# Extra matmuls into an unread PSUM bank while TensorE waits in two graph convolutions

## The chip, the cores and the metric

The kernel runs on one core of one Trainium2 chip. The metric is the device time of one execution, in microseconds (us), as the median of several runs.

## What is computed

Four graph layers stand one behind the other, on 6250 nodes with 128 features and 100000 edges that are sorted by their target. Each layer's result is added to its input and normalized over the features. The change lies in the fourth, two GCN convolutions with a relu between them:

```
def _gcn_layer(x, row, col, ew, W, b, n):
    deg = segment_sum(ew, col, num_segments=n)
    dis = where(deg > 0, rsqrt(maximum(deg, 1e-12)), 0.0)
    norm = dis[row] * ew * dis[col]
    h = x @ W
    msg = h[row] * norm[:, None]
    return segment_sum(msg, col, num_segments=n) + b

h = relu(_gcn_layer(x, row, col, ew, W1, b1, n))
out = _gcn_layer(h, row, col, ew, W2, b2, n)
x = layernorm(x + out)
```

The layers before it are an attention layer over the edges with a softmax (L0), one with four heads (L1), and an edge MLP (L2).

## The kernel before

The edges lie in 782 tiles of 128, the nodes in tiles of 128. Before each convolution a table `t3` or `t4` of all nodes' rows `dis * (x @ W)` is written to HBM. The convolution then does two things per edge: it fetches the row of the edge's source from the table, and it adds that row, times the edge weight, to the target's row.

The fetch is POOL's work. It issues one indirect DMA per tile of edges (line 2246, 128 rows of 128 floats), eight tiles to a group, 98 groups (`CTILE_GROUPS`), into a ring of 96 slots in SBUF (`conv_ring`, a part of `arena`). Before the gathers of group k, `landed` (line 1819) waits for group k - 2 and counts it in the semaphore `tiles_landed`; for the last groups `count_landed` (line 1812) does so.

The sum is PE's work. A step is one pair of a tile of edges and a tile of nodes that it touches; there are 832 such steps, in 104 groups of eight (`CSTEP_GROUPS`), which this document calls steps of PE where it speaks of one pass through `step`. PE multiplies a one-hot matrix of the targets (`hot8`, 128 x 128, with the edge weight as its one) with the fetched rows, and accumulates into one of three PSUM windows of 128 x 1024 floats (`pair[g % 3]`), at an offset that is read from a table. Each of the eight f32 matmuls shows as two records in the trace, 16 to a burst. Two small matmuls with zeros open the window (line 2290) and two close it (line 2299); the last one raises `summed`. PE waits for three things: that the window is cleared, that the one-hots are made, and that enough groups have landed, by a table `step_need` (lines 2289 to 2294).

DVE does four things per step: it builds the one-hots of the next step (TENSOR_SCALAR, line 2313, eight of them), adds the window to the accumulator of the nodes (TENSOR_TENSOR, line 2323), and clears the window (MEMSET, line 2326); the register of the first node is loaded ahead of them. ACT copies the next indices and weights (lines 2256 to 2261) once `summed` is raised, and raises `placed`. POOL's group k needs ACT's copies that were made at step k - 5 (`LAG`), so PE's and ACT's progress reaches POOL only at that distance.

Each engine's program is its own; semaphores alone tie them. `conv_rounds` (line 1798) writes the first twelve passes and the last eight out and makes a loop of twelve passes for those between. The bank `bank[7]`, the second half of `pair[3]`, is used by no engine in the two convolutions. The first one keeps a bias in the other half.

The constants are `ident_b`, the bf16 identity of 128 x 128, and `iota_b`, bf16 numbers 0 to 127 in each row.

Of the kernel before, what the change touches and what calls it, by code (L numbers as in the profile page):

```python
# [20 lines left out]
ALU = mybir.AluOpType  # L21
# [3 lines left out]
P = 128  # L25
# [19 lines left out]
CTILE_GROUPS = -(-ET // CG)  # L45
# [47 lines left out]
def build(nc, x, edge_i, edge_f, W_att_w, W_att_b, W1_w, W1_b, W2_w, W2_b, a_vec,  # L93
# [3 lines left out]
    with ctx:  # L97
        def sb(name, shape, dt=F32):
            return ctx.enter_context(nc.sbuf_tensor(name, shape, dt))
# [68 lines left out]
        iota_b = sb("iota_b", [P, P], BF16)  # L168
        ident = sb("ident", [P, P])
        ident_b = sb("ident_b", [P, P], BF16)  # L170
# [88 lines left out]
        bank = [pair[n // 2][:, (n % 2) * 512:(n % 2 + 1) * 512] for n in range(8)]  # L259
# [27 lines left out]
        v, s_, t_, q_ = nc.vector, nc.scalar, nc.tensor, nc.gpsimd  # L287
# [394 lines left out]
        def batch_rounds(eng, batch):  # L682

            batch(0, 0, 2)
            batch(1, 1, 2)
            with eng.Fori(2, NB - 2) as b:
                batch(b, 2, 2)
            batch(NB - 2, 2, 1)
            batch(NB - 1, 2, 0)  # L690

        NORM = BT + 1

# [50 lines left out]
        with nc.Block() as block:  # L744
# [301 lines left out]
            @block.tensor  # L1046
            def _(pe):
                turns = {at: (n, rows) for n, (at, rows, _) in enumerate(turned)}

                def turn(n, rows):  # L1050
# [51 lines left out]
        spare = wide[:, :, :, :].rearrange("p a b c -> p (a b c)")  # L1102
# [719 lines left out]

        def rows_of(eng, need, table, k):

            eng.reg_load([need], table[0:1, bass.ds(k, 1)])
            return eng.snap(need, min_val=0, max_val=CTILE_GROUPS - 1) + 1

        def at_least(eng, signal, k, more):

# [8 lines left out]
        with nc.Block() as block:  # L1838
# [134 lines left out]
            def _(dve):  # L1973
                first = [dve.alloc_register(f"l2_node{g}") for g in range(2)]
                slots = [dve.alloc_register(f"l2_slot{u}") for u in range(CG)]
                need = dve.alloc_register("l2_need")

                def hot_look(i, g, k):
                    dve.wait_ge(l2_rel_in[g % 4 // 2], 16 * (k // 4 + 1) if isinstance(k, int) else 4 * k - 4 * (g % 4) + 16)
# [253 lines left out]
        def convolution(name, table, table_out, also_act=None, also_dve=None):  # L2233
            placed, tiles_landed, hot_made, summed, added, cleared = (
                sem(f"{name}_{n}") for n in ("placed", "landed", "hot", "sum", "acc", "cleared"))
            with nc.Block() as block:
# [41 lines left out]
                @block.tensor  # L2278
                def _(pe):
                    slots = [pe.alloc_register(f"{name}_slot{u}") for u in range(CG)]  # L2280
                    offsets = [pe.alloc_register(f"{name}_offset{u}") for u in range(CG)]
                    need = pe.alloc_register(f"{name}_need")

                    def step(i, g, k):
                        window = pair[g % 3]
                        pe.reg_load(slots, step_slot[0:1, bass.ds(k * CG, CG)])
                        pe.reg_load(offsets, step_offset[0:1, bass.ds(k * CG, CG)])
                        pe.wait_ge(cleared, k + 1)
                        for h in range(2):
                            t_.matmul(window[:, h * 512:h * 512 + D], zeros[:, 0:P], zeros[:, 0:D], start=True, stop=False)  # L2290
                        pe.wait_ge(hot_made, k + 1)
                        pe.wait_ge(tiles_landed, rows_of(pe, need, step_need, k))
                        for u in range(CG):
                            slot = pe.snap(slots[u], min_val=0, max_val=CSLOTS - 1)
                            offset = pe.snap(offsets[u], min_val=0, max_val=CG - 1)
                            t_.matmul(window[:, bass.ds(offset * D, D)], hot8[:, g % 2, u, :], conv_ring[:, bass.ds(slot * D, D)],  # L2296
                                      start=False, stop=False)
                        for h in range(2):
                            last = t_.matmul(window[:, h * 512:h * 512 + 2], zeros[:, 0:P], zeros[:, 0:2], start=False, stop=True)  # L2299
                        last.then_inc(summed, 1)  # L2300

                    conv_rounds(pe, step, CSTEP_GROUPS)
# [210 lines left out]
```

## Time and profile before

| | |
|---|---|
| median of 3 runs | 6958.88 us |
| lowest, highest | 6939.15, 6967.73 us |
| profiled execution: span from its first to its last instruction | 5685.5 us |
| profiled execution: its own time | not recorded apart from its span |
| mean granted TensorE clock over the span | 0.647 |
| first convolution: first gather, last closing matmul | 3583.78, 4595.29 us |
| second convolution: last gather begins | 5631.8 us |

The median of the runs holds 1273 us that lie outside the span. Times in the trace count from the first instruction of the span. "PE" is a matmul on TensorE and "PEld" a weight load; "POOLq" is the instruction queue of GpSimd, in which its semaphore counts stand. PE, PEld, DVE, ACT and POOL overlap, and their shares are not to be added. The granted clock is given as a share of 2.4 GHz, so 0.50 is 1.2 GHz; a value between the two levels is a mean over a stretch in which it changed.

### The profile page before, as it was taken

What the parts mean: (1) busy time and instruction counts of PE and PEld (TensorE: products, weight loads), DVE (VectorE), ACT (ScalarE), POOL (GpSimd) and SP (SyncE); (2) the same over time, 40 slices, a digit from 0 to 9 for tenths busy, and PEclk for the clock granted to TensorE, in tenths of its full rate; (3) what the DMA queues carried; (4) which work ended last, traced back from release to release, by engine and by line L of the source; (5) the groups of instructions that cost most, each with busy time, mean ns of one, the idle gap of its engine ahead of it and who ended that gap; (6) DMA issues with size and microseconds to landing.
All of it is one profiled execution on the core that took longest, in us unless ns stands there. A gap on an engine that the chain in (4) does not pass through costs nothing. (4 is left out here: it accounts for less than half of the span.)

```text
span 5685.5 us, 82572 instructions
## 1 busy us (share of the span) xinstructions
PE 3113.8 (55%) x17051; PEld 2734.5 (48%) x17052; DVE 3263.6 (57%) x12090; ACT 1491.5 (26%) x5626; POOL 3958.0 (70%) x4054
## 2 busy tenths in 40 slices
PE   4444444356666666778898988433333443333333
PEld 3333333345555555657777776333333343333332
DVE  6888887676787787744444444433444443344445
ACT  2333333345555555532222223100000000000001
POOL 3777777736777777367777772677777757777774
PEclk7555555568888777865555556666666666666666
DMA  5111112214444444222121110111111121111112
GB/s 123 52 52 52 52 52 56 49 52 131 132 132 131 130 131 131 70 54 56 52 56 51 53 52 21 56 52 51 51 51 51 51 61 52 51 51 51 51 51 57
DMA packets 222234, 385.68 MB, mean 68 GB/s; under 512 B 85452, under 2 KB 121882, under 8 KB 221998
## 3 DMA queue, kind: packets, MB, share of 16 engines
q0 software_dynamic: 142944, 296.35, 19.0%
q1 hardware_dynamic: 79054, 86.72, 5.0%
q8 instruction: 83, 1.36, 0.1%
q14 instruction: 153, 1.25, 0.1%
HBM read 356.23 MB, written 26.56 MB: 67 GB/s over the span
## 5 line engine op out<-in xcount | busy, mean ns | idle before, releaser
L2246 POOL DMA_INDIRECT arena<-table_gcn,idx_now x1568 | 1532.2, 977 | 642.9 <-issue 422.1
L2296 PE MATMUL pair<-arena,hotf 128*128 x3328 | 726.6, 408 | 1224.7 <-POOLq L1819 1199.3
L2296 PEld LDWEIGHTS pair<-arena,hotf 128*128 128x128 f32 x3328 | 691.2, 317 | 1256.1 <-issue 1255.8
L664 POOL DMA_INDIRECT arena<-table_attention,idx_now x832 | 825.7, 992 | 272.7 <-issue 197.2
L664 POOL DMA_INDIRECT arena<-table_key_value,idx_now x832 | 789.2, 949 | 275.9 <-issue 221.1
L1852 POOL DMA_INDIRECT arena<-table_edge_mlp,idx_now x784 | 768.1, 980 | 261.2 <-issue 212.4
L2323 DVE TENSOR_TENSOR acc<-acc,pair 128x1024 f32 x208 | 253.9, 1221 | 1133.9 <-PE pair L2299 1133.9
L1069 PE MATMUL pair<-wide,hotf 128*128 128x130 f32 x1664 | 431.0, 439 | 653.3 <-ACT wide L1033 653.3
L1069 PEld LDWEIGHTS pair<-wide,hotf 128*128 128x128 f32 x1664 | 369.0, 326 | 718.5 <-ACT wide L1033 718.5
L2256 ACT COPY idx_now<-src_t 128x8 int32 (+1 forms) x204 | 39.3, 197 | 1815.2 <-PE pair L2299 1803.2
L1406 PE MATMUL pair<-wide,hotf 128*128 128x132 f32 x1664 | 314.1, 347 | 232.9 <-DVE acc L1436 232.8
L1991 DVE TENSOR_TENSOR hot<-pair,arena 128x64 f32<-128x64 f32 x832 | 132.8, 224 | 492.1 <-POOLq L1819 456.7
L2313 DVE TENSOR_SCALAR hotf<-iota,rel_now,ew_now 128x128 f32<-128x128 f32 x1664 | 406.5, 331 | 0.0
L1406 PEld LDWEIGHTS pair<-wide,hotf 128*128 128x128 f32 x1664 | 267.6, 241 | 272.9 <-issue 270.5
L1953 PE MATMUL pair<-wide,hotf 128*128 128x64 f32 x1664 | 373.8, 418 | 0.0
L1953 PEld LDWEIGHTS pair<-wide,hotf 128*128 128x128 f32 x1664 | 354.6, 324 | 6.5
L1397 PE MATMUL pair<-arena 128*128 x1664 | 307.6, 347 | 8.5 <-DVE arena L1453 8.5
L1397 PEld LDWEIGHTS pair<-arena 128*128 128x128 f32 x1664 | 293.2, 264 | 9.1 <-issue 8.9
L1349 ACT ACTIVATE junk<-iota,rel_now 128x128 f32<-128x128 f32 x832 | 265.7, 390 | 18.3 <-ACT idx_now L652 12.9
L1033 ACT ACTIVATE wide<-arena,small 128x129 f32<-128x129 f32 x832 | 267.0, 393 | 0.0
L1468 DVE TENSOR_TENSOR junk<-pair,arena 128x512 f32<-128x512 f32 x208 | 143.9, 692 | 204.4 <-DMA arena<-table_key_value,idx_now 204.2
L938 DVE SCALAR_TENSOR_TENSOR junk<-iota,rel_now,arena 128x128 f32<-128x128 f32 x832 | 256.4, 344 | 0.0
(371 smaller groups left out, 5709.7 us busy)
## 6 DMA issues: line engine op xcount, KB each, us to landing
key<-rel_dram SPq DMA_DIRECT2D x104, 256.0 KB, 3.4
arena<-rel_dram SPq DMA_DIRECT2D x52, 512.0 KB, 3.7
arena<-table_gcn,idx_now POOLq DMA_INDIRECT x1568, 2.5
arena<-table_attention,idx_now POOLq DMA_INDIRECT x832
arena<-table_key_value,idx_now POOLq DMA_INDIRECT x832
arena<-table_edge_mlp,idx_now POOLq DMA_INDIRECT x784, 2.4
table_attention<-arena SPq DMA_DIRECT2D x13, 512.0 KB, 3.0
table_gcn<-acc SPq DMA_DIRECT2D x26, 256.0 KB, 2.3
```

The lines of the kernel that those rows point to most:

```text
L664: q_.indirect_dma_start(ring[:, slot, 0:width], None, table, bass.IndirectOffsetOnAxis(ap=idx_now[:, slot:slot + 1].bitcast(U32), axis=0)) ...
L938: last = v.scalar_tensor_tensor(out=junk[:, 0, u * P:(u + 1) * P], in0=iota[:, :], scalar=rel_now[:, g * G + u:g * G + u + 1], in1=dst_sco ...
L1033: last = s_.activation(wide[:, g, u, 0:D + 1], ring[:, g * G + u, 0:D + 1], ACT.Identity, scale=small[:, g, u:u + 1])
L1069: last = t_.matmul(bank[2 * (g % 2) + u // 2][:, (u % 2) * AW:(u % 2) * AW + D + 2], hotf[:, g, u, :], wide[:, g, u, 0:D + 2], start=True, ...
L1349: last = s_.activation(away[:, u * P:(u + 1) * P], iota[:, :], ACT.Abs, scale=-1.0, bias=rel_now[:, g * G + u:g * G + u + 1])
L1397: last = t_.matmul(QB[g % 2][:, u * P:(u + 1) * P], hotT_f[:, g, u * P:(u + 1) * P], flat(look[:, bass.ds(nodes[u], 1), :]), start=True, s ...
L1406: last = t_.matmul(bank[SUM + 2 * (g % 2) + u // 2][:, (u % 2) * AW:(u % 2 + 1) * AW], hotf[:, g, u, :], wide[:, g, u, :], start=True, sto ...
L1852: q_.indirect_dma_start(mlp_ring[:, slot * EH:(slot + 1) * EH], None, t2, bass.IndirectOffsetOnAxis(ap=idx_now[:, slot:slot + 1].bitcast(U ...
L1953: last = t_.matmul(window[:, bass.ds(offset * EH, EH)], hot8[:, g % 2, u, :], s2[:, g % 2, u * EH:(u + 1) * EH], start=False, stop=(u == C ...
L2246: q_.indirect_dma_start(conv_ring[:, slot * D:(slot + 1) * D], None, table, bass.IndirectOffsetOnAxis(ap=idx_now[:, slot:slot + 1].bitcast ...
L2296: t_.matmul(window[:, bass.ds(offset * D, D)], hot8[:, g % 2, u, :], conv_ring[:, bass.ds(slot * D, D)], start=False, stop=False)
L2313: last = v.tensor_scalar(out=hot8[:, g % 2, u, :], in0=iota[:, :], scalar1=rel_now[:, at], scalar2=ew_now[:, at], op0=ALU.is_equal, op1=AL ...
```

## The change

A function `keep_busy(spare, times)` issues matmuls of `ident_b` with `iota_b` repeated four times (512 columns) into a bank that nobody reads. In both convolutions PE issues 24 of them in each step, behind the loads of its registers and ahead of its first wait. They do not enter the result. Beside that, `rows_of` takes two registers instead of one: it loads a number of a table into the first, and puts its maximum with 0 into the second. `rows_of` serves PE in the convolutions and DVE in the edge MLP.

```diff
+        def keep_busy(spare, times):
+
+            for _ in range(times):
+                t_.matmul(spare, ident_b[:, :], iota_b[:, :].unsqueeze(1).to_broadcast([P, 4, P]), start=True, stop=True)
...
         def rows_of(eng, need, table, k):
 
-            eng.reg_load([need], table[0:1, bass.ds(k, 1)])
-            return eng.snap(need, min_val=0, max_val=CTILE_GROUPS - 1) + 1
+            loaded, bounded = need
+            eng.reg_load([loaded], table[0:1, bass.ds(k, 1)])
+            eng.reg_alu(bounded, loaded, 0, ALU.max)
+            return eng.snap(bounded, min_val=0, max_val=CTILE_GROUPS - 1) + 1
...
-                need = dve.alloc_register("l2_need")
+                need = [dve.alloc_register(f"l2_need{n}") for n in range(2)]
...
-                    need = pe.alloc_register(f"{name}_need")
+                    need = [pe.alloc_register(f"{name}_need{n}") for n in range(2)]
 
                     def step(i, g, k):
                         window = pair[g % 3]
                         pe.reg_load(slots, step_slot[0:1, bass.ds(k * CG, CG)])
                         pe.reg_load(offsets, step_offset[0:1, bass.ds(k * CG, CG)])
+                        keep_busy(bank[7], 24)
                         pe.wait_ge(cleared, k + 1)
```

On PE, the first step of the first convolution reads like this in the kernel before. Semaphores are reused between stages and show their first names: `n1_c` is `cleared` here, `n1_factors` is `hot_made` and `n1_xn` is `tiles_landed`.

```order
L2286 TENSOR_LOAD hot
L2287 TENSOR_LOAD hotT
L2290 MATMUL pair<-wide 128x128 [waits n1_c]
L2290 MATMUL pair<-wide 128x128
L1825 TENSOR_LOAD hot [waits n1_factors]
L1826 ISA
L2294 ISA [waits n1_xn]
L2296 REGISTER_ALU
L2296 MATMUL pair<-arena,hotf 128x128
```

The same place on PE with the change, whose lines are numbered 6 to 8 higher:

```order
L2293 TENSOR_LOAD hot
L2294 TENSOR_LOAD hotT
L695 MATMUL pair<-iota_b,ident_b 128x512 x24
L2298 MATMUL pair<-wide 128x128 [waits n1_c]
L2298 MATMUL pair<-wide 128x128
L1831 TENSOR_LOAD hot [waits n1_factors]
L1832 ISA
L2302 ISA [waits n1_xn]
L2304 REGISTER_ALU
L2304 MATMUL pair<-arena,hotf 128x128
```

The 24 matmuls stand ahead of all three waits of the step and wait for nothing themselves. No other instruction moved, and the number of register instructions is the same.

## Rows read from the trace of the kernel before

**Rows 1.** The page: busy us (share of the span) and instructions of each engine.

```profile
PE 3113.8 (55%) x17051; PEld 2734.5 (48%) x17052; DVE 3263.6 (57%) x12090; ACT 1491.5 (26%) x5626; POOL 3958.0 (70%) x4054
```

**Rows 2.** Waits: engine, tile and line, whom it waited for: total us, times, longest.

```profile
PE pair L2296 <- POOLq L1819: 1199.3, 192, 12.2
...
POOL arena L2246 <- DMA arena<-table_gcn,idx_now: 55.2, 181, 0.3
...
PE pair L2296 <- POOLq L1812: 21.3, 4, 6.4
```

**Rows 3.** Timeline, one group: start, duration, engine, line, operation [idle before <-releaser].

```profile
3904.02 0.94 POOL L2246 DMA_INDIRECT arena<-table_gcn,idx_now  x1 [0.30 <-issue]
...
3904.28 3.57 PE L2296 MATMUL pair<-arena,hotf 128*128 x16 [6.41 <-POOLq L1819]
...
3907.78 0.20 PE L2299 MATMUL pair<-wide 1*128 1x2 bf16 x2
...
3908.13 1.22 DVE L2323 TENSOR_TENSOR acc<-acc,pair 128x1024 f32 x1 [5.96 <-PE pair L2299]
...
3909.01 0.95 POOL L2246 DMA_INDIRECT arena<-table_gcn,idx_now  x1 [0.30 <-issue]
3909.64 0.91 DVE L2326 MEMSET pair<- 128x1024 f32 x1 [0.29 <-DVE acc L2323]
3910.26 1.17 POOL L2246 DMA_INDIRECT arena<-table_gcn,idx_now  x1 [0.30 <-issue]
3910.46 1.95 DVE L2313 TENSOR_SCALAR hotf<-iota,rel_now,ew_now 128x128 f32<-128x128 f32 x8
3911.74 0.97 POOL L2246 DMA_INDIRECT arena<-table_gcn,idx_now  x1 [0.30 <-issue]
...
3914.26 0.95 POOL L2246 DMA_INDIRECT arena<-table_gcn,idx_now  x1 [0.31 <-issue]
```

**Rows 4.** Timeline, the gather ahead of the one-hots in an early and a late group.

```profile
3622.28 1.43 POOL L2246 DMA_INDIRECT arena<-table_gcn,idx_now  x1 [0.30 <-issue]
3622.74 1.95 DVE L2313 TENSOR_SCALAR hotf<-iota,rel_now,ew_now 128x128 f32<-128x128 f32 x8
...
4303.39 0.95 POOL L2246 DMA_INDIRECT arena<-table_gcn,idx_now  x1 [0.30 <-issue]
...
4303.78 1.95 DVE L2313 TENSOR_SCALAR hotf<-iota,rel_now,ew_now 128x128 f32<-128x128 f32 x8
```

**Rows 5.** Windows: stretch, length, busy us of PE, PEld, DVE, ACT, POOL, PEclk, DMA, GB/s.

```profile
3696.00:3838.00 142.00, 53.80 (x280) 50.00 (x280) 54.47 (x138) 5.65 (x42) 108.17 (x112) 0.66 0.18 52
...
3907.00:3907.50 0.50, 0.50 (x4) 0.50 (x4) 0.00 (x0) 0.00 (x0) 0.46 (x1) 0.50 0.25 66
...
3908.00:3908.50 0.50, 0.12 (x2) 0.00 (x0) 0.37 (x1) 0.39 (x3) 0.50 (x1) 1.00 0.49 131
...
3911.00:3911.50 0.50, 0.00 (x0) 0.00 (x0) 0.50 (x3) 0.00 (x0) 0.43 (x1) 0.50 0.01 0
```

**Rows 6.** Timeline, first gather and last three steps of the first convolution.

```profile
3583.78 0.94 POOL L2246 DMA_INDIRECT arena<-table_gcn,idx_now  x1 [126.09 <-ACT ew_now L2261]
...
4580.14 3.56 PE L2296 MATMUL pair<-arena,hotf 128*128 x16 [6.44 <-POOLq L1812]
...
4583.97 2.23 PE L2296 MATMUL pair<-arena,hotf 128*128 x16
...
4586.13 0.20 PE L2299 MATMUL pair<-wide 1*128 1x2 bf16 x2
...
4587.35 0.94 POOL L2246 DMA_INDIRECT arena<-table_gcn,idx_now  x1 [0.30 <-issue]
...
4591.60 3.75 PE L2296 MATMUL pair<-arena,hotf 128*128 x16 [4.11 <-POOLq L1812]
...
4595.29 0.21 PE L2299 MATMUL pair<-wide 1*128 1x2 bf16 x2
```

**Rows 7.** The bf16 matmul of 512 columns in the edge MLP: ns min/median/max.

```profile
L1937 PE MATMUL pair<-tab x104: 384/602/605, 2475.7 to 3471.6; 3*128 3x512 bf16 x104
```

## The prediction

> **What bounds the kernel now.** I read the busy times first [rows 1]: no engine is busy all the time, POOL comes nearest with 70%, PE has 55%. A share over the whole span says little of a change in two stages, so next come the waits [rows 2]. In the two graph convolutions PE waits 1199.3 us in 192 waits, 6.2 us each, for POOL's count of landed groups, and 4 times more for the counts at the end. POOL waits for none of them: 0.30 us pass between one gather and the next, put down to "issue" or, 181 times, to a DMA, at most 0.3 us each. So POOL, with its 784 gathers per convolution (98 groups of 8), sets the pace, and PE and DVE follow.
>
> One group in the middle of the first convolution shows the beat [rows 3]. Five gathers on from 3904.02 comes the one at 3910.26: they start every 1.248 us. The same place of the next group is at 3914.26: 10.24 us for eight. Eight times 1.248 is 9.98, so 0.26 us are lost. They are seen in the row at 3910.26, whose gather takes 1.17 instead of 0.94 (0.23), and in the next (0.03 to 0.04). PE starts its 16 matmul records 0.26 us after the gather at 3904.02, runs 3.57 us, and then DVE adds (3908.13), clears (MEMSET, 3909.64) and builds the next one-hot tiles (from 3910.46). The long gather began while the MEMSET ran, and ended 0.97 us after the one-hots began: it was held until the MEMSET was over. An earlier group [rows 4] says the same: with the gather 0.46 us ahead of the one-hots it takes 1.43, 0.49 more. The hold is that distance plus 0.03. In the other case there, 0.39 us ahead, there was no hold; I know no reason, and such cases are rare (a second, at the same kind of step, is the only other one I found). In all of the first convolution 783 gather intervals take 4587.35 - 3583.78 = 1003.6 us [rows 6]; at 1.248 us they would take 977.2. The loss is 26.4 us, 0.27 us for each of 97 groups. This is the one cost on POOL that PE's speed can move.
>
> The clock [rows 5]: the burst from 3904.28 on ran at a granted 0.50 (1.2 GHz), the level went to 1.00 (2.4 GHz) after 3907.5, when the burst was all but over, stayed there while PE idled, and was back at 0.50 at 3911. The mean over a stretch of the stage is 0.66. So nearly every burst runs at the lower level.
>
> **The change, part by part.**
>
> *The 24 added matmuls of each of 208 steps.* No row has this shape 24 times over. The nearest is the one bf16 matmul of 512 columns [rows 7]: 602 ns in the median, at the lower level, 384 ns at the least. The difference, 218 ns, is what halving the clock is worth, so the columns take about 215 ns at the upper level and 430 at the lower, and the rest is a fixed part that overlaps with the neighbours (the burst of [rows 3] puts a record every 0.22 us in 3.57 us for 16). A block is then 24 x 0.215 = 5.2 us at 2.4 GHz, and 24 x 0.43 = 10.3 at 1.2 GHz; with nothing overlapped 9.2 and 14.4. I take 5.2: the block begins right behind the previous burst, when the level has just gone up [rows 5], and is itself unbroken work. It lies in the wait of 6.2 us of [rows 2], and that wait grows by the 1.34 us below. It ends about 2.3 us before the next group lands. Cost in the steady state: nothing, covered by POOL's 10.2 us.
>
> *The real burst at 2.4 GHz.* The gap before it shrinks from 6.4 us to some 2.3. After a burst the level held for about 3 us of idling [rows 5], so it should mostly still be up. How long a burst takes then is in [rows 6]: the one at 4583.97 follows another directly, at the upper level, and its closing matmul (line 2299) starts 2.16 us after it, against 3.50 in [rows 3]. The gain is 1.34 us per step, and not on the path: nobody but DVE and ACT waits for it, and POOL reads ACT's counts five groups late.
>
> *What POOL gets of it.* DVE's three steps move forward by 1.34 us against the gathers: one-hots at 3909.12 instead of 3910.46, MEMSET from 3908.30. Now the gather that starts at 3909.01 falls into the MEMSET, 0.11 us before its end. The hold is 0.11 + 0.03 = 0.14 instead of 0.23, and 0.03 stays for the next: the period is 9.98 + 0.17 = 10.15. Against the mean loss of 0.27 that saves 0.10 us x 97 groups x 2 = 19 us. The bounds: a hold of 0 (the MEMSET ends before the gather starts) and one of 0.85 (it starts just ahead of it, the MEMSET's 0.82 us to the one-hots and 0.03). I take 0.14 because each distance in it has its row; it is a difference of times that all move together.
>
> *The ends.* Around the last gather of a convolution lie three steps [rows 6]: bursts at 4580.14 (ready then, after a wait), 4583.97 and 4591.60, the last when its group is counted. With blocks between them: closing matmul at 4582.30, block to 4587.6, burst to 4589.8, block to 4595.1, burst, closing matmul at 4597.3, where it was 4595.29. That is 2 us later, twice: +4 us. Twelve of the 208 steps did not wait for POOL (192 + 4 did, [rows 2]); there the block stands on PE's path and makes up to three steps late, but POOL is five groups away, so I count nothing.
>
> *The first step* has 12.2 us of idle PE ahead of its burst (the longest such wait): it hides a block even at the lower level (10.3). *The registers:* one load and one register operation per step stand in the order before and after, so the new bound replaces an operation, at no cost.
>
> [...]
>
> **Sum.** -19 + 4 = -15 us. The page gives one profiled execution, a span of 5685.5 us, and no time of its own; the runs have a median of 6958.88, 1273 us more, which I leave as it is. 6959 - 15 = 6944 us.
>
> **The rivals.**
> 1. *Nothing moves* (22%). The level falls in the remaining gap, so bursts end as before, or the hold belongs to the one-hots and follows them wherever they fall, at the size that it has. For it: work on PE and the upper level do not go together simply here, since an idle PE had 1.00 at 3908 [rows 5]. Time 6959 + 4 = 6963.
> 2. *The hold goes* (11%). Only 0.11 us separates the MEMSET's end from the gather's start. If DVE is 0.11 us earlier, 0.24 us x 194 = 47 us go: 6959 - 47 + 4 = 6916.
> 3. *A longer hold* (9%), the slow side in small: a burst only partly at 2.4 GHz is, say, 0.7 us faster instead of 1.34. Then the MEMSET starts at 3908.94, just before the gather at 3909.01, which is held 0.78. Over shifts from 1.34 down to 0.67 the hold averages 0.5, that is 0.27 more than now: x 194 = 52, so 7015; if all stay at 0.8, 7070. It decides as soon as the burst gains less than 1.3 us.
> 4. *PE becomes the bound* (5%), the slow side in large: the block runs at 1.2 GHz. A step is then 10.3 + 3.5 + 0.3 = 14.1 us, 104 steps 1466 us instead of the 1012 from the first gather to the last burst: +454 x 2, so 7870. It decides from 7.8 us per block on (10.24 less 2.16 and 0.3), 0.32 us per matmul. Against it: in [rows 5] the level rose over one unbroken burst, and the block is as unbroken and longer.
> 5. *PE's gain counts in full* (3%): 1.34 x 208 = 279 us, 6680. The Trainium skill (TensorE: Matmul & The Clock Gate, "Why this matters for your kernels") advises to keep TensorE busy without gaps for throughput, which is what the change does; whether the kernel gains is another thing. What speaks against this rival is that PE waits for POOL in all but twelve steps [rows 2].
>
> My forecast has 50%, with 6930 to 6965 as its own range.
>
> **Numbers.** 0.5% is 35 us, about what a measurement of this kernel tells from no change. Faster by more: most of rival 2, rival 5, a little of the forecast: 13%. Slower by more: rivals 3 and 4: 14%. Within: 73%. The range goes from 6910 (rival 2) to 6990 (rival 1 with the spread of the runs, 6939 to 6968, and the mild part of rival 3); rivals 4, 5 and the rest of 3 are left out.
>
> **What would show it.** In the profile of the changed kernel: PE busy up by 208 x 5.2 = 1080 us; the waits of PE for POOL about 2.3 us each instead of 6.2; the granted clock of the convolutions near 1 instead of 0.66; real bursts of 2.2 us; the fourth, not the fifth, gather behind a burst's start held, by 0.14; the distance of the same gather in two groups 10.15. If the bursts take 3.5 us, the second part is wrong; if the group takes 10.24 with short bursts, the account of the hold is wrong; if PE no longer waits for POOL, everything is.

## The result, and the profile after

| | before | with the change |
|---|---|---|
| median | 6959.17 us (4 runs) | 7133.07 us (4 runs) |
| lowest, highest | 6939.15, 6967.73 | 7125.05, 7141.42 |
| ratio of the medians, 95% interval | | 1.025, 1.0225 to 1.0274 |

The change costs 174 us where 15 us were to be gained. The time lies far outside the range. Of the changed kernel, time and profile agree: the profiled run took 7130.8 us, its span is 7129.0 us. The same holds for the kernel before: in the runs below, each of its times is 1.8 or 1.9 us above that execution's span. That settles one sentence ahead of the prediction: the 1273 us between the span of the profiled execution (5685.5) and the median do not lie outside the span. They lie inside the executions that were timed, and the execution that was profiled did not have them.

The page after has this row against [rows 1]:

```profile
PE 4410.4 (62%) x22043; PEld 3109.6 (44%) x22044; DVE 3294.8 (46%) x12090; ACT 1485.1 (21%) x5626; POOL 3939.3 (55%) x4054
```

PE has its 4992 more matmuls and is busy for 1297 us more. POOL does the same work in the same time, over a longer span. The waits of the convolutions, from 4500 us to the end, stand against [rows 2]:

```profile
ACT idx_now L2263 <- remote: 1874.1, 116, 50.2
DVE acc L2331 <- remote: 1393.2, 116, 46.3
POOL arena L2253 <- ACT ew_now L2268: 720.1, 115, 197.6
...
PE pair L695 <- issue: 297.5, 331, 5.7
...
PE pair L2304 <- issue: 232.6, 205, 5.2
```

The row "PE <- POOLq", 1199 us before, is gone: PE no longer waits for POOL, the sign by which the prediction would call everything in it wrong. POOL waits for ACT instead, 115 times; two of these waits are the starts of the convolutions, and the other 113, 409 us, are not in the profile of before. ("remote" stands where the profile does not tell which instruction ended the wait.) And PE has a kind of idle time of which the profile of before has next to none in these stages, "issue": nothing that the profile shows holds it. It comes to 596 us in the two convolutions, where the profile of before has 18. One stretch of the first convolution shows both (the columns of [rows 3]; the added matmuls are line 695, real ones 2304, closing ones 2307):

```profile
5041.19 1.72 PE L2304 MATMUL pair<-arena,hotf 128*128 x13
...
5043.62 0.27 PE L2304 MATMUL pair<-arena,hotf 128*128 x1 [0.71 <-issue]
5044.33 0.37 PE L2304 MATMUL pair<-arena,hotf 128*128 x1 [0.45 <-issue]
...
5046.47 0.27 PE L2304 MATMUL pair<-arena,hotf 128*128 x1 [1.76 <-issue]
5047.17 0.16 PE L2307 MATMUL pair<-wide 1*128 1x2 bf16 x1 [0.43 <-issue]
...
5049.28 0.16 PE L2307 MATMUL pair<-wide 1*128 1x2 bf16 x1 [1.95 <-issue]
...
5050.69 0.59 PE L695 MATMUL pair<-iota_b,ident_b 128*128 128x512 bf16 x1 [1.25 <-issue]
...
5052.80 0.59 PE L695 MATMUL pair<-iota_b,ident_b 128*128 128x512 bf16 x1 [1.52 <-issue]
5054.20 6.52 PE L695 MATMUL pair<-iota_b,ident_b 128*128 128x512 bf16 x22 [0.81 <-issue]
...
5055.26 1.22 DVE L2331 TENSOR_TENSOR acc<-acc,pair 128x1024 f32 x1 [15.06 <-remote]
...
5056.44 0.94 POOL L2253 DMA_INDIRECT arena<-table_gcn,idx_now  x1 [4.44 <-ACT ew_now L2268]
```

Read it from the top. The burst begins at full speed, 13 matmuls in 1.72 us; then matmuls come singly, 0.7 or 1.4 or 2.1 us apart, through the rest of the burst and into the added block, for some 11 us. Such a stretch is called a **pause** below. The granted clock, 1.00 when it began, was 0.50 from 5046.96 to 5057.20. DVE and ACT, which wait for `summed`, start at 5055.26, six us after the last closing matmul's record, and POOL has stood idle for 4.44 us when ACT's copies let it go on. Then PE runs its steps without a gap: from 5062.85 to 5070.46, closing matmul to closing matmul, is 7.61 us.

The end of that convolution shows such steps one behind the other:

```profile
5720.84 0.20 PE L2307 MATMUL pair<-wide 1*128 1x2 bf16 x2
5720.97 5.35 PE L695 MATMUL pair<-iota_b,ident_b 128*128 128x512 bf16 x24
5726.25 0.28 PE L2298 MATMUL pair<-wide 1*128 1x128 bf16 x2
5726.46 2.05 PE L2304 MATMUL pair<-arena,hotf 128*128 x16
...
5796.94 0.20 PE L2307 MATMUL pair<-wide 1*128 1x2 bf16 x2
```

The last gather began at 5711.0. PE was then more than ten steps behind and did ten of them in 76.1 us, 7.61 each.

### The profile page after: what moved, and what is told of

Same layout as the page of the kernel before. It is cut to its first block and busy times, and to the rows that moved or that the text cites. A ratio compares the mean times of both kernels' runs of the same rounds, so it can differ in the third digit from the quotient of the medians.

```text
span 7129.0 us, 92556 instructions
## 1 busy us (share of the span) xinstructions
PE 4410.4 (62%) x22043; PEld 3109.6 (44%) x22044; DVE 3294.8 (46%) x12090; ACT 1485.1 (21%) x5626; POOL 3939.3 (55%) x4054
## 3 DMA queue, kind: packets, MB, share of 16 engines
q8 instruction: 86, 1.41, 0.1%
## 5 line engine op out<-in xcount | busy, mean ns | idle before, releaser
L695 PE MATMUL pair<-iota_b,ident_b 128*128 128x512 bf16 x4992 | 1368.3, 424 | 307.2 <-issue 297.5
L664 POOL DMA_INDIRECT arena<-table_key_value,idx_now x832 | 815.5, 980 | 597.4 <-ACT idx_now L652 336.4
L695 PEld LDWEIGHTS pair<-iota_b,ident_b 128*128 128x128 bf16 x4992 | 498.4, 104 | 1086.1 <-issue 675.2
L1074 PEld LDWEIGHTS pair<-wide,hotf 128*128 128x128 f32 x1664 | 370.6, 327 | 979.4 <-ACT wide L1038 788.7
L1411 PE MATMUL pair<-wide,hotf 128*128 128x132 f32 x1664 | 356.8, 381 | 622.3 <-DVE acc L1441 378.7
L2304 PE MATMUL pair<-arena,hotf 128*128 x3328 | 514.3, 301 | 234.3 <-issue 232.6
L1411 PEld LDWEIGHTS pair<-wide,hotf 128*128 128x128 f32 x1664 | 307.3, 273 | 663.7 <-issue 662.5
L2304 PEld LDWEIGHTS pair<-arena,hotf 128*128 128x128 f32 x3328 | 446.1, 208 | 274.4 <-issue 255.4
L1960 PEld LDWEIGHTS pair<-wide,hotf 128*128 128x128 f32 x1664 | 352.2, 317 | 43.6 <-issue 37.2
L970 DVE TENSOR_TENSOR acc<-acc,pair 128x130 f32 x832 | 238.3, 286 | 246.0 <-remote 186.7
L1402 PE MATMUL pair<-arena 128*128 x1664 | 332.6, 368 | 8.5 <-issue 8.5
L1948 PE MATMUL pair<-we,tab 128*128 128x128 f32 x832 | 229.2, 428 | 124.5 <-issue 122.5
```

The source lines that it names most:

```text
L664: q_.indirect_dma_start(ring[:, slot, 0:width], None, table, bass.IndirectOffsetOnAxis(ap=idx_now[:, slot:slot + 1].bitcast(U32), axis=0)) ...
L695: t_.matmul(spare, ident_b[:, :], iota_b[:, :].unsqueeze(1).to_broadcast([P, 4, P]), start=True, stop=True)
L970: v.tensor_add(here, here, bank[2 * (g % 2) + u // 2][:, (u % 2) * AW:(u % 2) * AW + D + 2]).then_inc(l0_acc[u], 1)
L1074: last = t_.matmul(bank[2 * (g % 2) + u // 2][:, (u % 2) * AW:(u % 2) * AW + D + 2], hotf[:, g, u, :], wide[:, g, u, 0:D + 2], start=True, ...
L1402: last = t_.matmul(QB[g % 2][:, u * P:(u + 1) * P], hotT_f[:, g, u * P:(u + 1) * P], flat(look[:, bass.ds(nodes[u], 1), :]), start=True, s ...
L1411: last = t_.matmul(bank[SUM + 2 * (g % 2) + u // 2][:, (u % 2) * AW:(u % 2 + 1) * AW], hotf[:, g, u, :], wide[:, g, u, :], start=True, sto ...
```

## The experiments

Each kernel is the changed kernel with the edit shown, unless the text says otherwise; "before" is the kernel before, timed in turn with it on the same chip. The runs met six chips, and these turned out to be of two kinds, so each table names the time of the kernel before.

Two theories stood at first. *Occupancy*: the block fills the time in which PE used to catch up after a pause, so that its array time counts. *Supply*: each added instruction makes the pauses longer, so that the number counts.

### First: undo the block, and the size against the number

**The block taken out**, the registers' bound kept:

```diff
-                        keep_busy(bank[7], 24)
```

> The change without its matmuls: only the second register of rows_of stays. Both theories: the same time as before, 6959 +- 15 us (ratio 1.00). What its profile decides: the timed runs of before took 6959 us although the profile of before spans 5685.5. If the profile of this kernel spans some 6957 us and shows PE idle with 'issue' as the reason in every stage (as the profile of the change does, 1 us at a time), then those pauses of PE belong to the kernel as it is timed, and the profile of before simply had none. If it spans 5686, the change's matmuls brought the pauses.

**24 short matmuls**, 128 columns instead of 512:

```diff
-                t_.matmul(spare, ident_b[:, :], iota_b[:, :].unsqueeze(1).to_broadcast([P, 4, P]), start=True, stop=True)
+                t_.matmul(spare[:, 0:P], ident_b[:, :], iota_b[:, :], start=True, stop=True)
```

> 24 added matmuls per step as in the change, but of 128 columns instead of 512: the same number of instructions (10,000 more on PE), a quarter of the array time (block about 1.3 to 1.5 us at 2.4 GHz, up to 2.6 at 1.2, instead of 5.9). Theory occupancy (the block fills the wait in which PE used to catch up after a pause of its instruction stream, so pauses reach POOL through the copies of ACT): about before, 6959 to 6985 us. Theory supply (each added instruction makes PE's stream pause more): about the change, 7110 to 7140 us.

**6 long matmuls**, as many columns as 24 short ones:

```diff
-                        keep_busy(bank[7], 24)
+                        keep_busy(bank[7], 6)
```

> 6 added matmuls of 512 columns: the columns of e2, a quarter of the instructions. Theory occupancy: the same as e2, 6959 to 6985 us. Theory supply: a quarter of the change's loss, 6959 + 44 = 7003 us, well below e2.

| | time, us | before, us | ratio, 95% |
|---|---|---|---|
| no block | 6959.7 | 6958.6 | 1.0003, 0.9987 to 1.002 |
| 24 short | 7028.7 | 6958.6 | 1.010, 1.0074 to 1.0126 |
| 6 long | 6963.9 | 6958.6 | 1.0015, 1.000 to 1.003 |

The registers' part of the change costs nothing: the block is the whole loss. With the same columns, four times the matmuls cost 70 us against 5. With the same number of matmuls, four times the columns cost 174 against 70. So both theories fall as they were stated, and number and size each count. The 24 short ones and the 6 long ones even take the same time where PE does not pause: 1.50 and 1.51 us for the block.

The stages show where each counts. Against the kernel without a block, the 24 short matmuls make the two convolutions' gathers 73 us longer and the stretches behind the last gathers 7 us. The change makes the gathers 84 us longer and those stretches 75. So the number costs time among the pauses, and the size where PE works off what it is late.

The profile of the kernel without the block is the more telling find. It is the kernel before in all but the registers, its span is 6961.2 us, and its stages are all longer than in the profile that the prediction read. From the first gather to the last: the attention's take 1338 us instead of 1096, the edge MLP's 1263 instead of 1006, the first convolution's 1142.6 instead of 1003.6 [rows 6]. PE in the first convolution:

```profile
4993.63 0.77 PE L2303 MATMUL pair<-arena,hotf 128*128 x2 [1.34 <-issue]
...
5000.63 0.77 PE L2303 MATMUL pair<-arena,hotf 128*128 x2 [2.00 <-issue]
5002.73 0.77 PE L2303 MATMUL pair<-arena,hotf 128*128 x2 [1.33 <-issue]
...
5004.83 0.21 PE L2306 MATMUL pair<-wide 1*128 1x2 bf16 x2
...
5005.03 1.22 DVE L2330 TENSOR_TENSOR acc<-acc,pair 128x1024 f32 x1 [19.70 <-remote]
...
5010.22 3.75 PE L2303 MATMUL pair<-arena,hotf 128*128 x16 [3.47 <-DVE hotf L2320]
```

The pauses are there without any block. PE's waits for POOL, of which the prediction lived, have shrunk to a few:

```profile
PE pair L2303 <- DVE hotf L2320: 527.8, 66, 27.3
PE pair L2303 <- issue: 467.6, 361, 12.3
...
PE pair L2303 <- POOLq L1824: 237.2, 19, 14.6
```

19 waits with 237 us instead of 192 with 1199. The slack of 6.2 us in every step, which was to cover the block, exists only where there are no pauses. Nor are POOL's waits for ACT the block's doing alone: this kernel has 63 of them behind the starts, 285 us, where the changed one has 113 with 409.

The 66 waits for DVE's one-hots tell what limits PE when it catches up without a block:

```profile
5673.58 1.95 DVE L2320 TENSOR_SCALAR hotf<-iota,rel_now,ew_now 128x128 f32<-128x128 f32 x8
...
5676.30 2.21 PE L2303 MATMUL pair<-arena,hotf 128*128 x16 [1.61 <-DVE hotf L2320]
...
5677.76 1.95 DVE L2320 TENSOR_SCALAR hotf<-iota,rel_now,ew_now 128x128 f32<-128x128 f32 x8
```

DVE then needs 4.18 us for a step (one-hots to one-hots), and PE waits for it. So a block of 1.5 us finds room even there: with 6 long matmuls the step at the end of the convolutions stays at some 4.2 us, with 24 short ones it is 4.3. With 12 long ones (2.75 us) it is 5.02, with the change's 24 it is 7.61.

### Second: the curve

> 12 added matmuls of 512 columns in each step. Two theories of the loss. (S, supply) PE's instruction stream has pauses, and each added instruction makes them longer, whatever its size; 6 instructions cost 5 us and 24 short ones 70 us, so 12 should cost about 25 us, 6985 us. (C, catch-up) after each pause PE is some steps late and has to catch up; what counts is how much PE time a step needs beyond the real work, by the array too: a block of 12 takes 2.6 us at 2.4 GHz, half of the change's 5.2, and by a curve through 1.3 us (+5) and 5.2 us (+174) it should cost 35 to 60 us, 6995 to 7020 us.

```diff
-                        keep_busy(bank[7], 24)
+                        keep_busy(bank[7], 12)
```

> 48 added matmuls of 32 columns in each step: twice the change's instructions, an eighth of its columns. (S) twice the instructions of the run with 24 short ones, at least twice its loss: 140 us or more, 7100 us or later, and the pauses in PE's records of the added matmuls alone grow from 566 us to over 1000. (C) the array needs some 48 x 0.05 = 2.4 us for the block where nothing pauses: about as much as 12 of 512 columns, 35 to 60 us, if the pauses themselves stay as they are.

```diff
-                t_.matmul(spare, ident_b[:, :], iota_b[:, :].unsqueeze(1).to_broadcast([P, 4, P]), start=True, stop=True)
+                t_.matmul(spare[:, 0:32], ident_b[:, :], iota_b[:, 0:32], start=True, stop=True)
...
-                        keep_busy(bank[7], 24)
+                        keep_busy(bank[7], 48)
```

> The change's block in the first convolution alone. Both theories put the loss in each stage by itself: half of 174, so 7046 us, with the second convolution's gathers back at 1.458 us each and its end 87 us after its last gather, as without any block. If the added instructions did something to the whole program (code that lies elsewhere, pauses that move), the second convolution or the stages ahead would be slower too, and the time further from 7046.

```diff
-                        keep_busy(bank[7], 24)
+                        if name == "c1":
+                            keep_busy(bank[7], 24)
```

> The change's block of 24 matmuls in every fourth step alone, none in the other three: six per step in the mean, as in the run with six in each, which cost 5 us. (S) the same count, so the same cost, 0 to 10 us, 6965 us. (C) the mean need of PE is the same too, and a catch-up over several steps meets one block at most: 0 to 15 us. A third (L, length): what costs is one long block that comes between a late step and the next, by itself; then a quarter of the change's loss, 43 us, 7003 us.

```diff
-                        keep_busy(bank[7], 24)
+                        if g % 4 == 3:
+                            keep_busy(bank[7], 24)
```

| | time, us | before, us | lost | ratio, 95% |
|---|---|---|---|---|
| 12 of 512 columns | 7013.0 | 6955.2 | 58 | 1.0104, 1.0066 to 1.0143 |
| 48 of 32 columns | 7285.1 | 6955.2 | 330 | 1.0497, 1.0461 to 1.0532 |
| first convolution only | 7035.3 | 6955.2 | 80 | 1.0126, 1.0079 to 1.0173 |
| every fourth step | 6997.7 | 6955.2 | 42 | 1.0061, 1.0035 to 1.0088 |

Each theory in its new form, (S) and (C), has a hit and a miss: the 12 long ones cost what (C) said (58 us, 35 to 60 expected), the 48 small ones what (S) said (330 us, 140 or more expected), and each is far from the other's number.

The loss is local: in the kernel with the block in the first convolution, the second one's gathers take 1.457 us each, as without any block, and the first one's 1.516, as with the change (1.514). A quarter of the blocks costs a quarter of the loss (42 of 174), as the third theory said, and more than the 5 us of six matmuls in every step, though the interval is wide (24 to 61 us). The 48 smallest matmuls cost twice what 24 full ones do, although they are an eighth of the columns. Their profile shows why (line 695 again):

```profile
5005.15 0.98 PE L695 MATMUL pair<-iota_b,ident_b 128*128 128x32 bf16 x33 [0.93 <-issue]
5007.02 0.20 PE L695 MATMUL pair<-iota_b,ident_b 128*128 128x32 bf16 x2 [0.90 <-issue]
5007.75 0.18 PE L695 MATMUL pair<-iota_b,ident_b 128*128 128x32 bf16 x1 [0.53 <-issue]
5008.47 0.20 PE L695 MATMUL pair<-iota_b,ident_b 128*128 128x32 bf16 x1 [0.54 <-issue]
```

33 of them run in 0.98 us; then the pause sets in, and each 0.72 us brings one or two. What is left of the block is stretched like that until 5015.7, and then the real burst. An added matmul that meets a pause stretches it by some 0.7 us, however short it is. There is a second difference in this kernel: its queue for instructions moved 3.72 MB, against 1.41 with the change. How much of the 330 us that is was not taken apart; on a chip without pauses the same kernel moves the same 3.72 MB and loses 17 us in all (the third group).

### Third: other instructions, and two chips without pauses

**24 register operations** instead of the block (the register `idle` is loaded once, ahead of the steps):

```diff
-                        keep_busy(bank[7], 24)
+                        for _ in range(24):
+                            pe.reg_alu(idle, idle, 0, ALU.max)
```

```diff
-                            offset = pe.snap(offsets[u], min_val=0, max_val=CG - 1)
+                            offset = pe.snap(offsets[u], min_val=0, max_val=(CG - 1) * D)
-                            t_.matmul(window[:, bass.ds(offset * D, D)], hot8[:, g % 2, u, :], conv_ring[:, bass.ds(slot * D, D)],
+                            t_.matmul(window[:, bass.ds(offset, D)], hot8[:, g % 2, u, :], conv_ring[:, bass.ds(slot * D, D)],
```

> The other way round: no added matmul, and eight register operations fewer in each step than before (the column in the window is multiplied by 128 once, in the table, instead of by PE for each matmul). (S) fewer instructions meet the pauses: 6 matmuls more cost 5 us, so 8 operations fewer gain little, 0 to 25 us, 6935 to 6960 us, and the gathers come at under 1.458 us. (M) nothing, 6955 us.

| | time, us | before, us | ratio, 95% |
|---|---|---|---|
| 24 register operations | 5671.5 | 5672.0 | 0.9998, 0.9988 to 1.0007 |
| eight fewer | 5661.6 | 5672.0 | 0.9986, 0.9976 to 0.9995 |

These two say nothing of the theories, and more than any other run: the kernel before takes 5672 us here. On this chip the time is what the profile of before shows, and so are the stages: the convolutions' gathers take 1003.7 and 1003.9 us, and PE waits 192 times for POOL, 1207 us. The pauses belong to some chips, or to what goes on around them at the time, and not to the kernel. The 10 us of the second kernel are not in its convolutions, whose gathers take 1003.6 and 1004.1. In the profiles its first gather of the convolutions comes 18 us earlier than that of the other kernel (3556.9 against 3574.8); why is not shown.

So the change itself was run again:

> The change itself once more, beside the kernel before on the same chip. The two runs ahead of this one (24 register operations; eight fewer) met a chip on which the kernel before takes 5672 us instead of 6957, with none of the pauses in PE's records. Two outcomes tell apart what the loss of 2.5% hangs on. If this chip has the kernel before at 5672 us: (P, pauses) without them PE waits 6.2 us for POOL in each step, the block is covered, and the sum of the prediction holds, -15 us, 5657 us, 5640 to 5685 with its bounds. (B, block) if the block itself were too much for PE, the 174 us, or a good part of them, would be lost here too, 5750 to 5850 us. If it is a chip with the kernel before at 6957 us: 7133 us again, and nothing is told apart.

> The 48 matmuls of 32 columns, which cost 330 us where the kernel before takes 6955 us. On a chip with the kernel before at 5672 us: (P) 48 of them take 1.5 to 2.4 us of a wait of 6.2, so nothing, 5655 to 5690 us. (B) PE's instruction stream is too slow for them in itself: 100 us or more lost, 5770 us or later. On a chip with the kernel before at 6957 us: 7285 us again.

| | time, us | before, us | ratio, 95% |
|---|---|---|---|
| the change | 5653.6 | 5665.0 | 0.9978, 0.9968 to 0.9989 |
| 48 of 32 columns | 5681.8 | 5665.0 | 1.0036, 1.0025 to 1.0047 |

This was again a chip without pauses (another one). The change gains 11.4 us on it. The 48 short matmuls lose 17 us where they lost 330 on another chip. One group of the changed kernel there, to be laid beside [rows 3]:

```profile
3900.97 2.24 PE L2304 MATMUL pair<-arena,hotf 128*128 x16 [1.34 <-POOLq L1824]
...
3903.14 0.20 PE L2307 MATMUL pair<-wide 1*128 1x2 bf16 x2
3903.18 0.94 POOL L2253 DMA_INDIRECT arena<-table_gcn,idx_now  x1 [0.30 <-issue]
...
3903.49 1.22 DVE L2331 TENSOR_TENSOR acc<-acc,pair 128x1024 f32 x1 [5.90 <-PE pair L2307]
...
3904.27 5.34 PE L695 MATMUL pair<-iota_b,ident_b 128*128 128x512 bf16 x24 [0.93 <-issue]
...
3904.99 0.91 DVE L2334 MEMSET pair<- 128x1024 f32 x1 [0.29 <-DVE acc L2331]
3905.68 1.13 POOL L2253 DMA_INDIRECT arena<-table_gcn,idx_now  x1 [0.30 <-DMA arena<-table_gcn,idx_now]
3905.82 1.95 DVE L2321 TENSOR_SCALAR hotf<-iota,rel_now,ew_now 128x128 f32<-128x128 f32 x8
...
3909.54 0.28 PE L2298 MATMUL pair<-wide 1*128 1x128 bf16 x2
...
3911.20 2.24 PE L2304 MATMUL pair<-arena,hotf 128*128 x16 [1.38 <-POOLq L1824]
...
3913.37 0.94 POOL L2253 DMA_INDIRECT arena<-table_gcn,idx_now  x1 [0.31 <-issue]
```

The block takes 5.34 us, the burst 2.24 instead of 3.57, PE still waits 1.38 us for POOL, and the same gather comes 10.19 us later instead of 10.24. The clock of the middle of each convolution, against [rows 5] (PE busy, PEld, DVE, ACT, POOL, PEclk):

```profile
3600.00:4500.00 900.00, 728.12 (x4077) 419.24 (x4075) 368.23 (x923) 37.05 (x276) 685.15 (x706) 1.00 0.20 52
4700.00:5600.00 900.00, 734.16 (x4105) 422.42 (x4102) 371.57 (x930) 36.08 (x272) 684.84 (x707) 1.00 0.20 52
```

2.4 GHz throughout, where it was 0.66 to 0.68.

### Fourth: what the pauses count

> The change and the eight register operations fewer, together. On a chip with the kernel before at 5665 to 5672 us: the change gave -11 us there, all in the convolutions; the eight fewer gave -10 with nothing of it in the convolutions' gathers, so I expect the change's -11 in them and -5 to -20 in all, 5645 to 5665 us. On a chip with the kernel before at 6957 us (S): PE has about a quarter fewer instructions beside the block, and the catch-up is shorter: 7133 less 10 to 40 us, 7093 to 7123 us; (M) only matmuls and weight loads meet the pauses: 7133 us.

> 24 register operations in each step and no matmul, as before; the first time this met a chip without pauses and could tell nothing of them. On a chip with the kernel before at 6957 us: (S) 35 to 70 us lost, 6990 to 7030 us; (M) nothing, 6945 to 6975 us. On a chip without pauses: no difference again.

The first is the changed kernel with the edit of eight fewer; the second is the kernel with 24 register operations, unchanged. Both met a chip with pauses.

| | time, us | before, us | lost | ratio, 95% |
|---|---|---|---|---|
| the change and eight fewer | 7228.7 | 7071.9 | 157 | 1.0229, 1.0209 to 1.0249 |
| 24 register operations | 7075.7 | 7071.9 | 4 | 1.0004, 0.9988 to 1.002 |

24 register operations in each step cost nothing that can be measured, where 24 short matmuls cost 70 us. That is (M)'s number, but its mechanism is not shown: PE's idle time with "issue" at the opening and real matmuls, 648 us in the kernel without a block, is 971 us here (696.2 in 471 times and 275.0 in 128), the longer pauses that (S) expected, and its waits for DVE's one-hots and for POOL have shrunk from 765 us to 467. So register operations seem to lengthen the pauses too, by less than the slack that is left. The two kernels ran on different chips, and no run settles it.

Eight register operations fewer leave the ratio at 1.0229, within the 1.0195 to 1.0239 that (S) gives and not to be told apart from the change's 1.025. What (S) gave as the reason, a shorter catch-up, did not happen: the steps at the end take 7.61 us as in the change.

Of a matmul, then, is it the number or the array's work? Both edits use a row of zeros. The first is shown against the kernel with 48 matmuls of 32 columns:

```diff
-                t_.matmul(spare[:, 0:32], ident_b[:, :], iota_b[:, 0:32], start=True, stop=True)
+                t_.matmul(spare[:, 0:32], zeros[:, 0:P], zeros[:, 0:32], start=True, stop=True)
```

> 48 added matmuls of 32 columns as in the run that lost 330 us, but from one row of zeros instead of a full identity matrix: the same number of weight loads and matmuls, and almost nothing for the array to switch. On a chip with pauses: (N, number) the pauses meet each matmul or weight load, whatever is in it: again 300 to 350 us lost. (A, activity) the pauses answer to the array's work: well under 100 us lost. On a chip without pauses: 0 to 20 us lost, as the 17 us of the other.

The second is shown against the changed kernel:

```diff
-                t_.matmul(spare, ident_b[:, :], iota_b[:, :].unsqueeze(1).to_broadcast([P, 4, P]), start=True, stop=True)
+                t_.matmul(spare, zeros[:, 0:P], zeros[:, :], start=True, stop=True)
```

> The change's block, 24 matmuls of 512 columns, from one row of zeros instead of the full 128: the same time of the array for each, and almost nothing switched in it. On a chip with pauses: (N) the change's loss of 157 to 174 us; (A) less than half of it. On a chip without pauses: if the clock does not count such rows as work, the bursts stay at 1.2 GHz and the gain of 11 us is gone; if it does, 11 us gained.

| | time, us | before, us | lost | ratio, 95% |
|---|---|---|---|---|
| 48 of 32 columns, one row | 7457.1 | 7104.0 | 353 | 1.0499, 1.0447 to 1.0551 |
| 24 of 512 columns, one row | 7573.8 | 7104.0 | 470 | 1.0669, 1.0627 to 1.0711 |

The 48 lose the same 5.0% with one row of zeros as with a full identity: for these short ones the number counts, and not what is in them. The 24 long ones should then have lost 157 to 174 us and lost 470, for a reason that neither theory had:

```profile
5324.52 0.21 PE L2307 MATMUL pair<-wide 1*128 1x2 bf16 x2
5324.59 10.40 PE L695 MATMUL pair<-wide 1*128 1x512 bf16 x24
5334.78 0.41 PE L2298 MATMUL pair<-wide 1*128 1x128 bf16 x2
5335.13 3.78 PE L2304 MATMUL pair<-arena,hotf 128*128 x16
5338.84 0.21 PE L2307 MATMUL pair<-wide 1*128 1x2 bf16 x2
```

PE has no gap here, and next to none in both convolutions (153 us of "issue", against 596 with the change), and still the block takes 10.40 us, the burst 3.78, and the step 14.32: all of it at 1.2 GHz. The window of a whole millisecond in the first convolution (the columns of [rows 5]) has PE busy for 979 us of it, at a granted clock of 0.54:

```profile
5000.00:6000.00 1000.00, 979.13 (x3248) 509.30 (x3247) 294.75 (x738) 29.32 (x218) 506.58 (x535) 0.54 0.14 35
```

This is the prediction's fourth rival, nearly to the size: it had 10.3 for the block and 14.1 for the step. It happens to a block of one row of zeros and not to the change's block of 128 rows of constants, which has a granted clock of 0.82 in the like window on a chip with pauses (5000 to 6000 us there, 4600 to 5600 in the profile with the change). Rows and values were changed together, so no run tells which of the two keeps the clock down.

## Why the prediction was wrong

**The step that failed** is the one with the least working: the profile gives "a span of 5685.5 us, and no time of its own; the runs have a median of 6958.88, 1273 us more, which I leave as it is". With it falls "Cost in the steady state: nothing, covered by POOL's 10.2 us", since its cover, the wait of 6.2 us in [rows 2], was read from an execution that is not one of those timed. In the timed ones PE pauses again and again, POOL is no longer the only thing that sets the pace, and PE has to catch up after each pause. Without the block a step that catches up takes 4.16 us (eight steps end between 5670.90 and 5704.15 at the end of the first convolution), and DVE sets that; with the block PE sets it, at 7.61. The block measured 5.35 us, near the predicted 5.2: not its size was wrong but the wait that was to hide it, 6.2 us in each step by the prediction and none with the change.

Of the 174 us, the traces show two parts. From first to last gather, the convolutions take 1185.8 and 1182.3 us instead of 1142.6 and 1141.3: 84 us. POOL's waits for ACT's copies, which come late when PE is late, grow by more, from 285 to 409 us; the gathers that begin under a MEMSET lose less, 28 us against 54. After the last gathers, 114.2 us go by until the second convolution's first gather instead of 73.4, and 121.5 until the end instead of 87.5: 75 us (40.8 and 34.0), the backlog of about ten steps at 3.45 us more each, twice, and some more in the first. That is 159 of the 168 us between the two spans; the other 9 lie ahead of the first convolution.

**The same steps on a chip without pauses** can be judged by themselves (the profile of the changed kernel there, against those of the kernels without a block):

| the prediction's step | predicted | measured |
|---|---|---|
| block of 24 | 5.2 us | 5.34 |
| real burst, start to closing matmul | 2.16 | 2.17 |
| granted clock of the convolutions | near 1 | 1.00 |
| PE's wait for POOL | 2.3 | 1.4 |
| hold of the gather by the MEMSET | 0.14 | 0.19 |
| the group's period | 10.15 | 10.19 |
| gathers of both convolutions | -19 us | -11.5 |
| the ends | +4 us | -2 at the first, 0 at the second |
| sum | -15 us | -11.4 (medians of the runs) |
| PE busy | +1080 us | +847 |

The wait is 1.4 because a block starts 0.93 us after the closing matmul, where the prediction had it "right behind", and takes 0.14 us longer. PE's busy time rose by less than the 1080 us because that number has the blocks alone; the prediction's own shorter bursts, 1.34 us in each of 208 steps, take 279 us off it and give 801. The hold was 0.19 with the gather 0.14 us ahead of the one-hots: the rule "distance plus 0.03" is 0.02 short. The end of the first convolution is as predicted for PE (11.05 us from the last gather to the last closing matmul, 7.94 before: +3.1, where +2 was predicted), but the next stage then runs at 2.4 GHz from its first matmul (the granted clock is 1.00 up to 4607.32; in the profile of before it is 0.50 from 4590.19 to 4607.26, over the convolution's end and the first 12 us behind it), and from the last closing matmul to the next convolution's first gather it takes 27.3 us instead of 32.6: from the last gather to the next convolution's first are 38.3 us, and 40.5 in the kernel with eight operations fewer. The prediction did not look at that.

**The rule on shared access.** The hold still lies under the end of the MEMSET: in the profile of before 192 of the 197 gathers that begin during a MEMSET take 0.94 us plus, within 0.1 us, their distance to the one-hots, while those that begin under the one-hots take 0.97 us. The Trainium skill (SBUF — State Buffer, "Who interferes with whom") has DVE contend with GpSimd in its two-port modes, or with two inputs in SBUF while GpSimd's instruction reads SBUF; a MEMSET into PSUM is neither. There the trace and the skill differ, and the trace decides. The few gathers without a hold (four of them 0.38 to 0.39 us ahead of the one-hots) stay unexplained.

**The advice to keep TensorE fed** (the Trainium skill, TensorE: Matmul & The Clock Gate, "Why this matters for your kernels") worked for the clock, from 0.67 to 1.00, and was worth 0.2% on the chip without pauses.

**The rivals.** Rival 4 (PE becomes the bound) had the right engine and the right sign, and the wrong reason: it asked for a block of 7.8 us or more at 1.2 GHz. On the chips with pauses 5.3 us are enough, because the pauses had used the slack up. Its point of decision was computed from the same 10.24 us.

**What stays open.** What the pauses are. They are in PE's records of the kernels that were profiled on four chips (the kernel before at 6955 to 7104 us) and not on two (5665 and 5672); they come in all stages, matmuls come one or a few at a time, multiples of about 0.7 us apart, and `summed` reaches DVE and ACT up to some microseconds after the closing matmul's record. No run tells whether one chip changes between the two conditions, or whether the supply of instructions, another load on the chip or something else makes them. Whether register operations lengthen them is open as well, and so is whether it was the single row or the zeros that kept the clock of the last kernel down.

No version here is faster than the kernel before on both kinds of chip. On chips without pauses the change (0.9978) and the eight register operations fewer (0.9986) are, and the two cannot be told apart; on the others nothing was below the kernel before.

## What to carry to other kernels

If a profile's span and the timed runs differ by far more than other runs' do (1.8 us here), the profile shows another kind of execution than those that were timed. Then no wait in it is a slack to build on: find first which stages hold the difference, or bound every "hidden" term by what it costs without its cover. Work that is added to an engine "because it waits anyway" is free only as long as that engine is never late; once it is late, most of it stands on the path (3.45 of 5.35 us here), step after step, until it has caught up. For the same columns the filler with the fewest instructions was the cheapest here: six matmuls of 512 columns cost 5 us and 24 of 128 cost 70. And what hides such work need not be the wait that one sees: in the catch-up it was DVE's 4.18 us per step, which hid a block of 1.5 us and not one of 5.3.

## What I had not expected of the hardware

- The same kernel takes 5665 to 5672 us on some chips and 6955 to 7104 us on others, 23 to 25% more, and its runs on one chip lie within 0.7% of each other.
- On the latter PE's matmuls come singly, 0.7 us or a multiple apart, for 10 to 20 us at a time. 48 matmuls of 32 columns cost 5.0% from one row as from 128; 24 register operations cost nothing that could be measured.
- The granted clock stayed at 0.54 in a stretch in which PE was 98% busy with blocks of 24 matmuls from one row of zeros, and was 1.00 with the change's blocks from 128 rows of constants, with PE 81% busy. The two kernels differ in the operands alone (rows and values), but that 1.00 is from a chip without pauses; on one with pauses the change's blocks had 0.82, with PE 77% busy.
